# Attention scores from a 16-channel projection: projecting 2,048 columns at a time in four column tiles of 32

## What is computed

```python
xf = x.reshape(B, C, N)                                    # C = 256, N = 4096
f = jnp.einsum('kc,bcn->bkn', w1, xf) + b1[None, :, None]  # k = 16
energy = jnp.einsum('bkn,bkm->bnm', f, f)
attention = jax.nn.softmax(energy, axis=-1)
out = jnp.einsum('bcm,bnm->bcn', xf, attention)
x = x + out.reshape(B, C, H, W) * 0.1
```

## Time and profile before

| | |
|---|---|
| median of 3 runs | 1997.22 us (1996.63 to 1999.72) |
| the profiled execution | 1996.2 us, span 1994.3 us |
| mean granted clock of TensorE | 0.977 |
| PE busy | 1914.3 us, 96% |
| DVE busy | 1618.3 us, 81% |
| ACT busy | 1419.3 us, 71% |
| POOL busy | 1200.6 us, 60% |

### The profile page before, as it was taken

How to read it: one execution, slowest core, us unless ns; L and a number is a source line. 1 busy time by engine, 2 the same in 40 slices (tenths; PEclk the granted TensorE clock), 3 DMA queues, 4 the chain that set the end, 5 groups by cost and what they waited for, 6 DMA issues and landing times. The chain is left out here.

```text
span 1994.3 us, 40002 instructions
## 1 busy us (share of the span) xinstructions
PE 1914.3 (96%) x15232; PEld 1644.5 (82%) x15232; DVE 1618.3 (81%) x2151; ACT 1419.3 (71%) x2793; POOL 1200.6 (60%) x848
## 2 busy tenths in 40 slices
PE   6999999999999999999999999999999999989990
PEld 2789899998988899999899989998999999854440
DVE  5787888888888888888888888888888888777787
ACT  5777777778777777788777777788777777643335
POOL 4555555567755555567755556677655566477760
PEclk7899999999999999999999999999999999999995
DMA  6111111112211110122111110111011102433009
GB/s 213 40 50 61 53 38 35 31 64 67 81 40 50 59 40 32 32 72 95 53 60 57 40 40 23 56 57 53 32 32 32 32 30 77 170 145 120 1 35 387
DMA packets 58287, 133.67 MB, mean 67 GB/s; under 512 B 9328, under 2 KB 9328, under 8 KB 57584
## 3 DMA queue, kind: packets, MB, share of 16 engines
q1 hardware_dynamic: 58096, 131.10, 19.3%
HBM read 84.48 MB, written 33.62 MB: 59 GB/s over the span
## 5 line engine op out<-in xcount | busy, mean ns | idle before, releaser
L750 POOL CAST Ph<-P 128x1024 fp32r<-128x1024 f32 x496 | 722.6, 1457 | 641.4 <-ACT P L508 641.4
L519 ACT ACTIVATE scw<-scw,nb 128x512 f32<-128x512 f32 (+1 forms) x988 | 656.1, 664 | 345.4 <-DVE nb L600 345.2
L600 DVE TENSOR_REDUCE nb<-scw 128x1 f32<-128x512 f32 (+1 forms) x988 | 678.7, 689 | 255.7 <-PE scw L410 250.7
L428 PE MATMUL accb<-Ph,xh 64*128 64x512 f32 x2048 | 807.4, 394 | 1.3 <-ACT tb L529 1.3
L428 PE MATMUL acct<-Ph,xh 64*128 64x512 f32 x2048 | 807.4, 394 | 0.0
L428 PE MATMUL accb<-Ph,xl 64*128 64x512 f32 x2048 | 800.4, 391 | 0.0
L428 PE MATMUL acct<-Ph,xl 64*128 64x512 f32 x2048 | 796.5, 389 | 0.0
L610 DVE TENSOR_TENSOR Pl<-P,Ph 128x1024 fp32r<-128x1024 f32 x512 | 674.6, 1318 | 20.4 <-ACT Ph L513 15.9
L428 PE MATMUL acct<-Pl,xh 64*128 64x512 f32 x2048 | 635.4, 390 | 0.0
L428 PE MATMUL accb<-Pl,xh 64*128 64x512 f32 x2048 | 632.2, 388 | 0.0
L508 ACT ACTIVATE P<-ee 128x1024 f32<-128x1024 f32 x512 | 526.1, 1028 | 61.5 <-PE ee L401 39.7
(11 more groups left out here) (145 smaller groups left out, 1418.4 us busy)
## 6 DMA issues: line engine op xcount, KB each, us to landing
wk<-xt SPq DMA_DIRECT2D x32, 512.0 KB, 3.8
xres<-x SPq DMA_DIRECT2D x32, 512.0 KB, 3.9
x<-xres SPq DMA_DIRECT2D x32, 512.0 KB, 2.8
R<-rd SPq DMA_DIRECT2D x32, 256.0 KB, 3.1
xn<-x SPq DMA_DIRECT2D x16, 512.0 KB, 12.3
xr<-x SPq DMA_DIRECT2D x16, 512.0 KB, 9.9
out<-xr SPq DMA_DIRECT2D x16, 512.0 KB, 10.2
An<-x SPq DMA_DIRECT2D x14, 512.0 KB, 5.2
```

The costliest lines, as they stand in the source:

```text
L428: return pe.matmul(to[:, :], w[rows, g * GM + k, c * 128:(c + 1) * 128], p[rows, s, k * QC:(k + 1) * QC], start=g == 0 and i == 0, stop=g ...
L519: nc.scalar.activation(to, to, ACT.Exp, bias=nb[:, t % 2, w:w + 1], accum_out=bsum[:, t % 2, w:w + 1]).then_inc(bsum_done, 1)
L600: nc.vector.tensor_reduce(nb[:, t % 2, w:w + 1], of, AX.X, ALU.max, negate=True).then_inc(nmax_done, 1)
L750: nc.gpsimd.tensor_copy(Ph[:, e % RP, :], P[:, e % 2, :]).then_inc(ph_done, 1)
```

## The change

A projection now takes four pieces of x and makes 2,048 columns, in four column tiles of 32 output rows (rounded and remainder only): FQ = 32, FJ = 4, FU = 2 projections per image. The third group of rows is a second DMA of the first 16 rows. The rows of ones are written once to both T buffers by DVE at the start. T's upper and lower halves are filled by separate calls of `f_rows`, each with eight DMAs (four of 32 rows, four of 16). In the start-up image 0 is projected at scan steps 0 and 4, unit 0 waits for all of the first call's DMAs and unit 8 for the second's, and SP's order is rewritten. In the steady part a projection stands at group 5 of tiles 2 and 4, its upper rows at group 8 and its lower rows at group 13.

```diff
-FU = N // (2 * FW)
+FQ = 2 * KF
+FJ = 128 // FQ
+FU = N // (FJ * FW)
...
-        HEAD_F = {0: (0, 1, 2), 4: (3,)}
-        HEAD_HL = {0: (0, 1), 2: (2,), 4: (3,)}
+        HEAD_F = {0: (0,), 4: (1,)}
+        HEAD_HL = {0: (0,), 4: (1,)}
...
-            if t >= 0 and b < NB - 1 and 1 <= q <= FU and g == 5:
-                return (b + 1) * FU + q - 1
+            if t >= 0 and b < NB - 1 and q in (2, 4) and g == 5:
+                return (b + 1) * FU + q // 2 - 1
...
-                    sp.wait_ge(f_filled, 2 * ((s - XP) // 2 + 1))
+                    sp.wait_ge(f_filled, FJ * ((s - XP) // FJ + 1))
...
-            def f_rows(s):
+            def f_rows(s, base, landed_in):
                 b, k = divmod(s, FU)
                 if b >= 2:
                     sp.wait_ge(e_done, (b - 1) * CH * G)
+                if s == 0:
+                    sp.wait_ge(ones_done, 2)
                 sp.wait_ge(hl_done, s + 1)
-                for base, landed_in in ((S0, ts_in), (0, te_in)):
-                    for j in range(2):
-                        at = (2 * k + j) * 512
-                        sp.dma_start(T[b % 2][base:base + KS, at:at + 512].bitcast(F32),
-                                     hl[s % 2][j * S0:j * S0 + KS, :]).then_inc(landed_in[s % 2], 16)
+                for j in range(FJ):
+                    at = (FJ * k + j) * 512
+                    for row, rows in ((0, FQ), (FQ, KF)):
+                        sp.dma_start(T[b % 2][base + row:base + row + rows, at:at + 512].bitcast(F32),
+                                     hl[s % 2][j * FQ:j * FQ + rows, :]).then_inc(landed_in[s % 2], 16)
...
             scan_rows(0)
-            f_rows(0)
+            f_rows(0, S0, ts_in)
+            load_xt(0)
             scan_rows(1)
-            for s in range(1, FU):
-                f_rows(s)
-                load_xt(s - 1)
+            load_xt(1)
+            f_rows(1, S0, ts_in)
+            load_xt(2)
+            for s in range(FU):
+                f_rows(s, 0, te_in)
             load_res(0)
...
                     if g == 8 and t >= 0 and projected(t, 5) is not None:
-                        f_rows(projected(t, 5))
+                        f_rows(projected(t, 5), S0, ts_in)
+                    if g == 13 and t >= 0 and projected(t, 5) is not None:
+                        f_rows(projected(t, 5), 0, te_in)
...
             def project(s, bank):
-                for k in range(2 * s, 2 * s + 2):
+                for k in range(FJ * s, FJ * s + FJ):
                     pe.wait_ge(xp_in[k % XP], 16 * (k // XP + 1))
                 for c in range(CT):
-                    for j in range(2):
-                        mm = pe.matmul(bank[j * S0:(j + 1) * S0, 0:512], w1s[:, c, :], xp[(2 * s + j) % XP][:, c, :],
+                    for j in range(FJ):
+                        mm = pe.matmul(bank[j * FQ:(j + 1) * FQ, 0:512], w1s[:, c, :], xp[(FJ * s + j) % XP][:, c, :],
                                        start=c == 0, stop=c == CT - 1)
...
-                    if u < G and u % 4 == 0:
-                        pe.wait_ge(ts_in[u // 4 % 2], 32 * (u // 8 + 1))
+                    if u in (0, G // FU):
+                        pe.wait_ge(ts_in[u // (G // FU)], 32 * FJ)
...
+            for k in range(2):
+                nc.vector.memset(T[k][FQ:KS, :].bitcast(F32), 1.0).then_inc(ones_done, 1)
             dve.wait_ge(col_in, 16)
             dve.wait_ge(fill_done, 3)
```

More of the change, by code:

```diff
@@ L134, in attention @@
         hl = [xn[:, 1, (4 + k) * FW:(5 + k) * FW] for k in range(2)]
-        w1s = xn[:, 1, 6 * FW:6 * FW + CT * 64].rearrange("p (c k) -> p c k", c=CT)
+        w1s = xn[:, 1, 6 * FW:6 * FW + CT * FQ].rearrange("p (c k) -> p c k", c=CT)
         xp = [t[:, k * 2048:(k + 1) * 2048].bitcast(F32).rearrange("p (c n) -> p c n", c=CT)
@@ L152, in attention @@
         fill_done = sem("fill_done")
+        ones_done = sem("ones_done")
         xp_in = [sem(f"xp_in{k}") for k in range(XP)]
@@ L267, in f_rows @@
                     sp.wait_ge(e_done, (b - 1) * CH * G)
+                if s == 0:
+                    sp.wait_ge(ones_done, 2)
                 sp.wait_ge(hl_done, s + 1)
-                for base, landed_in in ((S0, ts_in), (0, te_in)):
-                    for j in range(2):
-                        at = (2 * k + j) * 512
-                        sp.dma_start(T[b % 2][base:base + KS, at:at + 512].bitcast(F32),
-                                     hl[s % 2][j * S0:j * S0 + KS, :]).then_inc(landed_in[s % 2], 16)
+                for j in range(FJ):
[3 more added lines that the diff above has]
+                                     hl[s % 2][j * FQ:j * FQ + rows, :]).then_inc(landed_in[s % 2], 16)
             def scan_rows(t):
                 b, q = divmod(t, CH)
-                s = b * FU + q // 2
+                s = b * FU + q // FJ
                 if t < 2:
@@ L280, in scan_rows @@
                 else:
-                    sp.wait_ge(ts_in[s % 2], 32 * (s // 2 + 1))
+                    sp.wait_ge(ts_in[s % 2], 32 * FJ * (s // 2 + 1))
                 if t >= 2:
@@ L285, in scan_rows @@
                 if t < 2:
-                    src, row, s = hl[0], t * S0, slice(0, QC)
+                    src, row, s = hl[0], t * FQ, slice(0, QC)
                 else:
                     src, row, s = T[b % 2].bitcast(F32), S0, slice(q * QC, (q + 1) * QC)
-                for to, at in ((0, 0), (1, 2), (2, 1)):
+                for to, at in ((0, 0), (1, 0), (2, 1)):
                     sp.dma_start(U[t % 2][S0 + to * KF:S0 + (to + 1) * KF, :].bitcast(F32),
@@ L446, in _ @@
                         for k in range(2):
-                            pe.wait_ge(te_in[k], 32 * (e // (G * CH) + 1) * FU // 2)
+                            pe.wait_ge(te_in[k], 32 * FJ * (e // (G * CH) + 1))
                     if held[0]:
@@ L456, in _ @@
                         pe.wait_ge(us_in[u // G % 2], 48 * (u // G // 2 + 1))
-                    if u < G and u % 4 == 0:
-                        pe.wait_ge(ts_in[u // 4 % 2], 32 * (u // 8 + 1))
+                    if u in (0, G // FU):
+                        pe.wait_ge(ts_in[u // (G // FU)], 32 * FJ)
                     elif u % (G * CH) == 0:
                         for k in range(2):
-                            pe.wait_ge(ts_in[k], 32 * (u // (G * CH) + 1) * FU // 2)
+                            pe.wait_ge(ts_in[k], 32 * FJ * (u // (G * CH) + 1))
                 if 0 <= e < NG:
@@ L531, in copy_f @@
             def copy_f(s, bank):
-                act.wait_ge(f_filled, 2 * (s + 1))
+                act.wait_ge(f_filled, FJ * (s + 1))
                 if s >= 2:
                     act.wait_ge(hl_done, s - 1)
-                nc.scalar.activation(Fp[s % 2][0:S0 + KS, :], bank[0:S0 + KS, 0:512], ACT.Identity,
-                                     bias=col[0:S0 + KS, 0:1]).then_inc(fp_done, 1)
+                nc.scalar.activation(Fp[s % 2], bank[:, 0:512], ACT.Identity, bias=col[:, 0:1]).then_inc(fp_done, 1)
             act.wait_ge(fill_done, 1)
@@ L583, in split_f @@
                 dve.wait_ge(fp_done, s + 1)
-                rows = slice(0, S0 + KS)
-                nc.vector.tensor_copy(f1[s % 2][rows, :].bitcast(F32R), Fp[s % 2][rows, :]).then_inc(f1_done, 1)
+                nc.vector.tensor_copy(f1[s % 2].bitcast(F32R), Fp[s % 2]).then_inc(f1_done, 1)
                 dve.wait_ge(f1_done, s + 1)
                 if s >= 2:
-                    dve.wait_ge(ts_in[s % 2], 32 * (s // 2))
-                    dve.wait_ge(te_in[s % 2], 32 * (s // 2))
+                    dve.wait_ge(ts_in[s % 2], 32 * FJ * (s // 2))
+                    dve.wait_ge(te_in[s % 2], 32 * FJ * (s // 2))
                 if s == 2:
@@ L592, in split_f @@
                     dve.wait_ge(us_in[1], 48)
-                nc.vector.scalar_tensor_tensor(hl[s % 2][rows, :].bitcast(F32R), f1[s % 2][rows, :], col[rows, 1:2],
-                                               Fp[s % 2][rows, :], ALU.mult, ALU.add).then_inc(hl_done, 1)
+                nc.vector.scalar_tensor_tensor(hl[s % 2].bitcast(F32R), f1[s % 2], col[:, 1:2], Fp[s % 2],
+                                               ALU.mult, ALU.add).then_inc(hl_done, 1)
             def block_max(v, of):
@@ L787, in _ @@
                 if t == NT - 2 and g == 4:
-                    pool.wait_ge(f_filled, 2 * NB * FU)
+                    pool.wait_ge(f_filled, FJ * NB * FU)
                     for k in range(2):
@@ L1095 @@
     w1, b1, w = (np.asarray(a) for a in (L0_conv_w1, L0_conv_b1, L1_conv_weights))
-    w1r = np.zeros((C, 64), f32)
+    w1r = np.zeros((C, FQ), f32)
     cols = np.zeros((128, 2), f32)
-    for r, low in enumerate((0, 1, 0)):
-        w1r[:, r * KF:(r + 1) * KF] = w1.T
-        for base in (0, S0):
-            rows = slice(base + r * KF, base + (r + 1) * KF)
+    for low in range(2):
+        w1r[:, low * KF:(low + 1) * KF] = w1.T
+        for j in range(FJ):
+            rows = slice(j * FQ + low * KF, j * FQ + (low + 1) * KF)
```

(3 more changed lines are left out.)

## The result

The changed kernel takes 2004.32 us (median of 6 runs, 2003.52 to 2005.62) against 1996.59 us of the kernel before in the same job (6 runs): 7.7 us slower, ratio 1.0039 with a 95% interval of 1.0029 to 1.0049. The forecast was slower by 4.4 us; sign and range held.

The account below looks back on a forecast made before the run. TensorE's back-to-back matmuls bound the steady part, GpSimd's chain the start-up. 1996.2 - 11.7 (steady part) + 16.1 (start-up) = 2000.6 us profiled, 2001.6 us as a median; own range 1998 to 2007, whole range 1994.5 to 2010.

Parts of the forecast that it names:

- project 1 split: Start-up: projection between scans from 29.9 us, with its copy and split taking 5.7 us, done at 35.6 us.
- GpSimd's halves end: Start-up: ten halves of 1.90 us from 56.5 us end at 75.5 us, where it was 59.44.
- Issue price: SyncE's queue in the start-up: each short T-row DMA taken at 0.62 us, next to the 16-row row.
- Rival C: Start-up: short DMAs are issued cheaply, at 0.36 us; 8.3 us come off, 1993.3 us; chance 0.12.
- Landing of block 3: Start-up: xt block 3 lands 4.5 us after its issue at 52.0 us, so at 56.5 us.
- Four column tiles: Steady projections: four tiles keep the four rounds of two, with 0.1 us added, 2.15 us per projection.
- Rivals A and B: Steady projections: A, column tiles run two at a time, 2019.6 us; B, four together but slower, 2007 us; chance 0.12 each.
- What set the start before: Start-up: GpSimd's chain, not the row sums, sets the start; first P ready 2.5 us before GpSimd came to it.
- The reserve path: Start-up: row sums through the shift rows to the first P, about 71.8 us, under GpSimd's 75.5; late next.
- The ones: VectorE at the start: two writes of 4096 columns, 3.8 us each, 7.5 for both; counted as zero cost.
- The loss: Start-up: GpSimd's halves end at 75.5 us instead of 59.44, 16.1 us lost.
- the gain: Steady part: six of 12 projections go, 24.6 us before and 12.9 us after, 11.7 us won.

Follow-up runs that it names:

- the run of the steady part alone: Changed kernel with image 0 put back to the form and issue order of the kernel before; 1984.33 us, ratio 0.9935 to the kernel before.

## Why the prediction was right, point by point

The chain was followed in the right order, and its terms came out so (us from the span's start):

| step | forecast | measured |
|---|---|---|
| project 0 starts | 10.4 | 10.97 |
| first scan-row issue | 16.3 | 16.65 |
| first scan | 25.0 | 25.12 |
| project 1 split | 35.6 | 36.39 |
| block 3 issued | 52.0 | 53.31 |
| block 3 used | 56.5 | 59.44 |
| GpSimd's halves end | 75.5 | 78.41 |

- **Issue price.** 0.62 us was taken from the 16-row row; 4.95 / 8 and 9.99 / 16 both give 0.62 us, for 32 and 16 rows mixed. Rival C, cheap short DMAs, falls: these 32 did not come near 0.48.
- **Landing of block 3.** The mis-sized term: 4.5 us were taken between 3.8 and 5.9, 59.44 - 53.31 = 6.1 us passed, 1.6 us more. Blocks 4 and 5 and the xres load were issued within 1.2 us around it; that they shared the transfer is argued, not tried.
- **The rest of the start-up.** 1.3 us more up to block 3's issue, half of it from one rounding on VectorE that took 1.09 us where it had taken 0.43. With the landing this makes the 2.9 us by which GpSimd ended later than forecast. GpSimd was idle twice, as forecast, but the longer of the two waits was the first, 11.17 us before block 2, and not the one before block 3, 9.08 us.
- **Four column tiles.** Rivals A and B fall at the 3.67 us between scans; the 0.1 us that I added per projection wasn't there. Term by term the steady gain is 12 x 2.05 - 6 x 2.04 = 12.4 us against 11.7 forecast; the run of the steady part alone gave 13.1 us, of which its profile has 1.0 us ahead of the first attention matmul.
- **What set the start before.** The prediction says that GpSimd's chain set it and not the row sums, since the first P was ready 2.5 us before GpSimd came to it. That reading was wrong: the two chains meet at the first attention matmul and not at the first P, and there the energies came last, by some 0.4 us. The forecast lost little by it: GpSimd's end moved by 19.0 us, the first attention matmul by 18.6.
- **The reserve path.** The forecast had the row sums 3.7 us ahead of GpSimd, by the first P. The first P was ready at 73.74 us (72.72 + 1.02), 4.7 us ahead of 78.41:

```profile
72.72 1.02 ACT L518 ACTIVATE P<-ee 128x1024 f32<-128x1024 f32 x1 [9.04 <-PE ee L411]
```

  At the attention, where the chains meet, the reserve was smaller: TensorE waited 1.63 us for GpSimd.

- **The ones.** 3.47 us per memset against 3.8 forecast, over by 9.4 us, while VectorE's next work begins at 15.41 us: no cost.
- **What the forecast left out.** Behind the start 11.2 us were won instead of 12.4. From the first to the last attention matmul it was 12.1 us (1697.3 against 1709.4 us), although more of it ran at the lower clock: at the granted clock of 0.50 (1.2 GHz) the attention matmuls ran on for 6.2 us after the first (to 85.70 us), and for 4.4 us before; the busy times in windows of the changed kernel and of the one before (engines, then PEclk):

```profile
79.50:85.40 5.90, 5.71 (x24) 3.64 (x26) 4.99 (x5) 3.14 (x7) 1.97 (x2) 0.50 0.00 1
85.60:90.00 4.40, 4.40 (x40) 3.71 (x39) 2.83 (x4) 2.84 (x6) 1.60 (x1) 0.99 0.00 0
```

```profile
60.90:65.30 4.40, 4.21 (x20) 2.61 (x18) 4.40 (x5) 2.13 (x4) 0.94 (x2) 0.50 0.02 5
```

In both TensorE had been running attention matmuls, with short waits, before the clock rose. 1.8 us more at half pace are about 0.9 us. Another 0.9 us were lost behind the last attention matmul (224.9 against 224.0 us), in the part that the change leaves as it was and that took 224.0 to 226.6 us in the nine profiles; what makes it vary stays open. Together that is somewhat more than the missing 1.2 us.
- **No luck in the sum.** The loss was forecast 2.5 us too small (16.1 for 18.6) and the gain 0.5 us too large (11.7 for 11.2). Both errors point the same way, so the right sign is not owed to errors that cancel.

## What to carry to other kernels

Two halves of one edit can pay with opposite signs: wider batches can halve a per-batch cost on the bound engine in the steady part, but the first batch also needs twice its inputs and twice its copies before anything can start, so run each half alone. In a start-up with one issuing queue, price every DMA by its issue, follow the queue in order to the load that the slowest chain waits for, and put short copies that are needed late behind the loads that are needed early. Where two chains race, compare them at the instruction that needs both: here the first attention matmul, and not the first P. A batch size can differ between the first image and the others.

## What was not expected

A DMA of 32 or 16 rows costs the queue 0.62 us, four fifths of the 0.79 us of 50 rows, so that splitting off the third copy was paid more per DMA than per byte: 32 issues of image 0 took 19.9 us of the queue (4.95 + 4.94 + 9.99). And four column tiles with four separate moving operands ran in the same time as two, 3.67 against 3.68 us between scans. Nor was it seen beforehand that in the kernel before two chains reached the first attention matmul within some 0.4 us of each other.
